# Three threshold searches of a top-k feed-forward layer: keys from PSUM, work moved into the rounds, one unit for the upper half

## The reference, cut to what matters

```python
input_acts_seq = gelu(einsum('bsd,nd->bsn', x, input_patterns)).mean(axis=1)     # (8, 2048)
top_input_acts, top_input_idx = top_k(input_acts_seq, 256)
input_repr = zeros((B, 2048)).at[brow, top_input_idx].set(top_input_acts)
process_acts = gelu(einsum('bn,pn->bp', input_repr, process_input_weights))      # (8, 1024)
top_process_acts, top_process_idx = top_k(process_acts, 128)
process_weights = softmax(top_process_acts, axis=-1)
aggregated_value = einsum('bk,bkd->bd', process_weights, process_values[top_process_idx])
output_acts_seq = gelu(einsum('bd,od->bo', aggregated_value, output_input_weights))   # (8, 2048)
top_output_acts, top_output_idx = top_k(output_acts_seq, 256)
out_per_seq = einsum('bk,bkm->bm', top_output_acts, output_patterns[top_output_idx])
x = x + tanh(g_ffn[1]) * broadcast(out_per_seq)
```

## Time and profile before

| | |
|---|---|
| median of 3 runs | 554.09 us (553.89 to 556.86) |
| profiled execution: time | 558.86 us |
| profiled execution: span, first to last instruction | 557.1 us |
| busy in the span | PE 377.0, DVE 380.4, ACT 264.1, POOL 105.8 us |
| mean granted TensorE clock | 0.825 of full |

### The profile page before, as it was taken

One profiled execution on the slowest core, in us unless ns is written; L12 is line 12 of the kernel. 1 busy time (PEld: TensorE's weight loads), 2 busy tenths in 40 slices (PEclk: granted clock), 3 DMA queues, 4 the chain that ended last, 5 costly groups with the idle time before them and its releaser, 6 DMA issues.

```text
span 557.1 us, 9426 instructions
## 1 busy us (share of the span) xinstructions
PE 377.0 (68%) x3000; PEld 251.6 (45%) x3004; DVE 380.4 (68%) x1614; ACT 264.1 (47%) x672; POOL 105.8 (19%) x384
## 2 busy tenths in 40 slices
PE   2899799912228699976998798898999601703006
PEld 2558576611116465563566566676545300203003
DVE  6643999989993767897887376581454576185773
ACT  3853544542222366545576375777453353253540
POOL 6694000000006239300495040000000000000000
PEclk9999599955556979999999798899999955855556
DMA  9800002459300597700759877900993000000002
GB/s 270 251 1 2 0 2 74 148 100 173 86 1 18 140 138 144 165 1 8 133 104 141 144 126 114 223 15 2 384 384 99 0 1 2 0 1 2 1 0 66
DMA packets 38585, 51.00 MB, mean 92 GB/s; under 512 B 5960, under 2 KB 35081, under 8 KB 37385
## 3 DMA queue, kind: packets, MB, share of 16 engines
q1 hardware_dynamic: 38537, 50.41, 38.9%
HBM read 40.28 MB, written 9.97 MB: 90 GB/s over the span
## 4 chain that ended last, share of the span: by engine, by line
PE 34%; DVE 33%; ACT 11%; DMA 7%; SPq 5%; issue 5%; POOL 4%; DVEq 0%; ACTq 0%; POOLq 0%
PE ps L2239 8%; DVE PR L1115 5%; ACT below L1829 5%; PE ps L2071 4%; DMA key_parts<-kp 4%; DVE R L1049 3%; PE ps L2016 2%; DVE below L1452 2%; DVE prod L1111 2%; PE ps L1932 2%; SPq L614 2%; SPq L628 2%; PE ps L2363 2%; PE ps L2189 2%; DVE PR L1113 2%
## 5 line engine op out<-in xcount | busy, mean ns | idle before, releaser
L1329 DVE TENSOR_REDUCE negm<-ps 112x1 f32<-112x375 f32 x128 | 64.0, 543 | 28.1 <-PE ps L2178 27.5
L1797 ACT ACTIVATE E<-ps 125x448 f32<-125x448 f32 x96 | 49.4, 546 | 28.1 <-PE ps L2189 26.1
L830 POOL CAST kp<-kx 128x188 bf16<-128x188 f32 (+1 forms) x32 | 10.6, 374 | 161.6 <-ACT path L1675 122.3
L1317 DVE TENSOR_REDUCE acts<-gel 128x4 f32<-128x448 f32 x32 | 19.8, 621 | 30.9 <-ACT gel L1761 30.9
L2203 PE MATMUL ps<-E,v 125*32 125x112 f32 x768 | 31.9, 274 | 5.8 <-issue 5.7
L2330 PE MATMUL ps<-cnt,same 128*128 128x7 bf16 (+1 forms) x22 | 3.6, 166 | 47.1 <-ACT below L1829 43.6
L2178 PE MATMUL ps<-ks,qs 96*112 96x375 bf16 x96 | 31.7, 347 | 4.0 <-DMA ks<-key_parts 2.9
L2189 PE MATMUL ps<-qs,ks 99*125 99x112 bf16 x288 | 30.5, 232 | 4.3 <-ACT E L1797 2.0
L2189 PEld LDWEIGHTS ps<-qs,ks 99*125 99x125 bf16 x288 | 27.2, 146 | 11.1 <-ACT E L1797 7.7
L1761 ACT ACTIVATE gel<-ps 128x448 f32<-128x448 f32 x32 | 17.3, 544 | 29.3 <-PE ps L2239 29.3
L1115 DVE TENSOR_TENSOR_SCAN PR<-UU,PR,prod 128x94 bf16<-128x94 bf16 x63 | 26.1, 414 | 2.2
(11 more groups left out here) (384 smaller groups left out, 1046.7 us busy)
## 6 DMA issues: line engine op xcount, KB each, us to landing
piwT<-fn_process_input_weights SPq DMA_DIRECT2D x4, 2048.0 KB, 17.0
ks<-key_parts SPq DMA_DIRECT2D x36, 187.5 KB, 7.9
key_parts<-kp SPq DMA_DIRECT2D x48, 93.8 KB
ctx_again<-in_ctx SPq DMA_DIRECT2D x7, 512.0 KB
keys<-kx SPq DMA_DIRECT2D x16, 187.5 KB, 2.0
kx<-keys SPq DMA_DIRECT2D x8, 375.0 KB, 7.1
ks_last<-key_parts SPq DMA_DIRECT2D x12, 187.5 KB, 6.8
ctxP<-in_ctx SPq DMA_DIRECT2D x8, 256.0 KB, 6.2
```

Of the source, the lines that this page charges most:

```text
L1317: dve.tensor_reduce(a0[:, i % NIT // 4, HB * half:HB * half + HB, i % 4], gel[:, i % 2, :].rearrange("p (b s) -> p b s", b=HB), AX.X, ALU. ...
L1329: drain(dve.tensor_reduce(negm[:, n:n + 1], bank(nm)[0:S, 0:SC], AX.X, ALU.max, negate=True), nm)
L1797: drain(fn(E[:, (KCH * f + c) % 6, :], bank(nm)[0:KC, 0:4 * S], ACT.Exp), nm)
```

## The change

The change touches the three searches alone. It does five things:

1. The copy of the transposed activations to `aT` is taken off the way to the keys: `sgn` and `key` read PSUM directly. Search 0 still makes the copy, in the wait of its round 0; search 1 makes none, since it never uses `aT`. The limits in `most` and the first `bound` are set before the activations are waited for.
2. The lower bits (`low`, `klo`) are made in the wait of round 0, not before the first round.
3. `khi` is stored in units of the lowest key bit (times 2^LOW), and so are `bound` and the candidates of the upper half. `kval` then is one instruction, (`khi` - `bound`) + `klo`.
4. The first candidates of the lower half come from a tile of their own, `low_cand`, written in the wait of round 1.
5. The softmax maximum of search 1 is spread over the waits of rounds 0, 1, 2 and 4 of that search, and its two PE instructions stand behind the counts of rounds 0 and 2. ACT's exponential moves behind ACT's tests of all rounds of search 1.

```diff
+                did(dve.memset(bound[:, :], -float(2 ** 31)))
                 if k < 2:
-                    nm = ("actT", k)
-                    wait_filled(dve, nm)
-                    drain(dve.tensor_copy(aT[:, :], bank(nm)[:, 0:128]), nm)
-                    wait_drained(dve, nm)
+                    turned_acts = ("actT", k)
+                    wait_filled(dve, turned_acts)
+                    bits = bank(turned_acts)[:, 0:128].bitcast(I32)
...
-                did(tt(key[:, :], sgn[:, :], bits, ALU.bitwise_xor))
+                ins = tt(key[:, :], sgn[:, :], bits, ALU.bitwise_xor)
...
                 did(dve.tensor_single_scalar(sgn[:, :], key[:, :], LOW[k], ALU.arith_shift_right))
-                did(dve.tensor_single_scalar(low, key[:, :], 2 ** LOW[k] - 1, ALU.bitwise_and))
-                settle()
-                did(dve.tensor_copy(khi[:, :], sgn[:, :]))
-                did(dve.tensor_copy(klo[:, :], low))
+                settle()
+                did(ts(khi[:, :], sgn[:, :], unit, None, ALU.mult))
                 settle()
                 first = sum(ROUNDS[:k])
-                ts(cand[:, 0:n], table(0)[0], -float(2 ** (31 - LOW[k])), None, ALU.add).then_inc(cand_ready, 1)
+                ts(cand[:, 0:n], table(0)[0], unit, -float(2 ** 31), ALU.mult, ALU.add).then_inc(cand_ready, 1)
                 dve.wait_ge(cand_ready, first + 1)
+
+                def beside(r):
+
+                    if r == 0:
+                        did(dve.tensor_single_scalar(low, key[:, :], 2 ** LOW[k] - 1, ALU.bitwise_and))
+                        settle()
+                        did(dve.tensor_copy(klo[:, :], low))
+                        if k == 0:
+                            drain(dve.tensor_copy(aT[:, :], bank(turned_acts)[:, 0:128]), turned_acts)
+                    if r == 1:
+                        lowest = [e[0] for e in rounds(k)].index(1)
+                        did(ts(low_cand[:, 0:n], table(lowest)[0], table(lowest)[1], None, ALU.mult))
+                    if k != 1:
+                        return
+                    if r == 0:
+                        dve.wait_ge(acts_ready, 2)
+                        dve.tensor_reduce(pmx[:, :], cells(acts[1], NPT), AX.X, ALU.max).then_inc(pmx_ready, 1)
+                    if r == 1:
+                        wait_filled(dve, "pmaxT")
+                        drain(dve.tensor_reduce(pm8[:, :], bank("pmaxT")[0:B, 0:128], AX.X, ALU.max), "pmaxT")
...
                 for r, (half, width, mine, theirs, last) in enumerate(rounds(k)):
...
-                    if half == 1 and r and rounds(k)[r - 1][0] == 0:
-
-                        did(ts(kval[:, :], khi[:, :], bound[:, 0:1], float(2 ** LOW[k]), ALU.subtract, ALU.mult))
-                        settle()
-                        val = kval[:, :]
-                        did(tt(val, val, klo[:, :], ALU.add))
-                        did(dve.memset(bound[:, :], 0.0))
-                        settle()
-                        ts(cand[:, 0:n], table(r)[0], table(r)[1], None, ALU.mult).then_inc(cand_ready, 1)
-                        dve.wait_ge(cand_ready, first + r + 1)
+                    if half == 1 and rounds(k)[r - 1][0] == 0:
+
+                        val, tried = kval[:, :], low_cand
+                        stt(val, khi[:, :], bound[:, 0:1], klo[:, :], ALU.subtract, ALU.add).then_inc(cand_ready, 1)
+                        dve.wait_ge(cand_ready, first + r + 1)
+                        did(dve.memset(bound[:, :], 0.0))
...
+                    beside(r)
                     nm = ("count", k, r)
                     wait_filled(dve, nm)
```

More of the change, by code:

```diff
@@ L423, in build_program @@
         nextb = r1.take("nextb", [128, 8])
+        low_cand = r1.take("low_cand", [128, 8])
         cnt = r1.take("cnt", [128, 8], BF16)
@@ L1432, in largest @@
+                if k == 1:
+                    drain(ins, turned_acts)
+                    wait_drained(dve, turned_acts)
+                else:
+                    did(ins)
+                    settle()
+                did(dve.tensor_single_scalar(sgn[:, :], key[:, :], LOW[k], ALU.arith_shift_right))
+                settle()
+                did(ts(khi[:, :], sgn[:, :], unit, None, ALU.mult))
                 settle()
                 first = sum(ROUNDS[:k])
-                ts(cand[:, 0:n], table(0)[0], -float(2 ** (31 - LOW[k])), None, ALU.add).then_inc(cand_ready, 1)
+                ts(cand[:, 0:n], table(0)[0], unit, -float(2 ** 31), ALU.mult, ALU.add).then_inc(cand_ready, 1)
@@ L1459, in largest @@
                         units, scale = table(r + 1)
-                        did(ts(nextb[:, 0:n], units, scale, bound[:, 0:1], ALU.mult, ALU.add))
+                        did(ts(nextb[:, 0:n], units, scale if half else scale * unit, bound[:, 0:1], ALU.mult, ALU.add))
+                    beside(r)
                     nm = ("count", k, r)
@@ L1517, in _ @@
                 drain(ins, nm)
[L1518 to L1523, removed]
-            ts(pmd[:, :], ident[0:B, 0:B], pm8[:, 0:1], None, ALU.mult).then_inc(pmd_ready, 1)
-            wait_filled(dve, "pmaxb")
-            drain(tt(cells(esel, NPT), cells(acts[1], NPT),
-                     bank("pmaxb")[:, 0:B].unsqueeze(2).broadcast_to([128, B, NPT]), ALU.subtract), "pmaxb")
             largest(1, B * NPT, NP // 8)
@@ L1826, in signs @@
                 val = kval if half else khi
+                tried = low_cand if half and rounds(k)[r - 1][0] == 0 else cand
                 with nc.allow_low_precision(reason="sums of signs up to 128 are exact"):
                     for m in range(mine, mine + theirs):
-                        ins = fn(below[:, m, :], val[:, :], ACT.Sign, bias=cand[:, m:m + 1], scale=-1.0,
+                        ins = fn(below[:, m, :], val[:, :], ACT.Sign, bias=tried[:, m:m + 1], scale=-1.0,
                                  accum_out=cnt[:, m:m + 1])
@@ L1846, in _ @@
             load_table(ACT.Exp)
+            for r in range(ROUNDS[1]):
+                signs(1, r)
             wait_drained(act, "pmaxb")
             fn(esel[:, :], esel[:, :], ACT.Exp).then_inc(pexp_ready, 1)
-            for r in range(ROUNDS[1]):
-                signs(1, r)
             load_table(ACT.Gelu)
@@ L2373, in _ @@
                 fill(ins, nm)
-            claim(pe, "pmaxT")
-            pe.wait_ge(pmx_ready, 1)
-            fill(tr(bank("pmaxT")[0:B, 0:128], pmx[:, :], ident[:, :]), "pmaxT")
-            claim(pe, "pmaxb")
-            pe.wait_ge(pmd_ready, 1)
-            fill(mm(bank("pmaxb")[:, 0:B], ones[0:B, :], pmd[:, :], start=True, stop=True), "pmaxb")
             act_transpose(1)
@@ L2382, in _ @@
                 count(1, r)
+                if r == 0:
+                    claim(pe, "pmaxT")
+                    pe.wait_ge(pmx_ready, 1)
+                    fill(tr(bank("pmaxT")[0:B, 0:128], pmx[:, :], ident[:, :]), "pmaxT")
+                if r == 2:
+                    claim(pe, "pmaxb")
+                    pe.wait_ge(pmd_ready, 1)
+                    fill(mm(bank("pmaxb")[:, 0:B], ones[0:B, :], pmd[:, :], start=True, stop=True), "pmaxb")
             ties(1)
```

25 lines of the change are left out of this document (16 added, 9 removed).

## The result

The changed kernel took 548.61 us (median of 4 executions, 545.3 to 550.58), the kernel before 554.71 in the same comparison (4, 553.89 to 556.86). The ratio is 0.988 with a 95% interval of 0.9838 to 0.9922. The forecast was 4.1 us, a ratio of 0.9926. Over all comparisons, this one included, the changed kernel has a mean of 549.6 us (23 executions) and the kernel before 554.6 (116): 5.0 us less, give or take 1.1 (95%, from the scatter of the single executions), about 0.9%. Three executions far outside the others, at 580 to 973 us, are left out here and in all means.

What follows compares the result with a forecast made beforehand. No engine alone but the dependent chain through the searches was taken to bound the kernel. Savings 1.45 + 1.47 + 1.55 less 0.35 lost gave 4.12 us; 554.09 - 4.1 = 550.0 us, range 548.2 to 552.2.

Steps and rivals of the forecast that it cites:

- A, keys: Key steps ahead of each search's first test: 0.55, 0.55 and 0.35 us saved, 1.45 in all, between 1.03 and 1.69.
- The surcharge for PSUM: Keys of searches 0 and 1: reading PSUM adds 0.06 us each to `sgn` and `key`.
- B, switch: From `bound` to the first lower test, each search: 1.07 us becomes 0.58, saving 0.49 three times, 1.47 in all.
- C, softmax maximum: Between `acts` and search 1: the wait of 2.03 us becomes 0.48, so search 1 starts 1.55 us earlier.
- The table load: ACT's load for Exp ahead of search 1: stays hidden by 0.40 us; the rival that it shows had under 0.02.
- D, the waits: Work moved into DVE's waits: 0.20 us lost in search 0, 0.1 and 0.05 in search 1; 0.35 in all.
- Rival 2: Clock rise in product L2363 shifts by 3 us: 1.5 us either way, 551.5 or 548.5; spread L2426 likewise; chance 0.20.
- L: Follow-up theory, not forecast: clock rises in product and end meet the shorter tail better, about 1 us beyond the searches' 4.4.
- S: Follow-up theory, not forecast: only the searches got faster, 4.4 us; the rest is scatter between executions.
- T: Follow-up theory, not forecast: the change gains more than its parts in every execution, first put at 6 to 8 us.
- d/2: Product L2363: a clock rise d later after the product's start costs d/2, since half speed does half the work.

Runs made afterwards that it cites:

- shared_out: Changed kernel with search 0's copy moved to the wait of round 2 and the `klo` cast to round 3; ratio 0.9883 to the kernel before.
- the delays: Settings of an unused tile ahead of search 0: eight in the kernel before, ratio 1.003; twelve in the changed kernel, ratio 0.9954.
- the first control: The kernel before, unaltered, under a label of its own (also written control); ratio 1.0052 to the kernel before, mean 556.8 us beside 553.6.
- again2: The changed kernel, unaltered, timed a third time; ratio 0.9909 to the kernel before.
- before_late: The kernel before with eight settings of an unused tile ahead of the first key step of search 0; ratio 1.003 to the kernel before.

## Why the prediction fell short

*A, keys.* Foreseen 0.55, 0.55 and 0.35; measured 0.61, 0.61 and 0.34. The surcharge for PSUM was taken twice and holds once. The Trainium skill, "VectorE: DVE Perf Modes", "The perf-mode tier table (the rule you actually need)", says that two-tensor operations on fp32 have only the slowest mode, in SBUF too. `key`, on int32 of the same width, fits that: it stayed at 0.29. The higher fixed cost of PSUM that the prediction cited does not show in `key`, and against the 0.20 us for each search that it estimated from those figures stand 0.06 measured.

*B, switch.* Foreseen 0.49 three times, measured 0.49, 0.48 and 0.49.

*C, softmax maximum.* Foreseen 1.55, measured 1.55 (2.03 to 0.48). The table load stayed hidden, by 0.34 us.

*D, the waits.* Foreseen 0.20, 0.10 and 0.05; measured 0.19, 0.09 and 0. shared_out shows that even these can be had back.

*Sum.* Foreseen 4.12, measured 4.44 in the searches. 0.11 of the difference is in A and 0.07 in D, 0.01 the other way in B. Of the remaining 0.15, 0.09 are in round 9 of search 0, where a pause of DVE moved behind the candidates (last section); the rest is spread over hundredths. Each step of the mechanism was right, and the sizes to a few hundredths.

*What failed is the step from the sum to the time:* "the stretches used above do not scale with it, so I take 4.1 off the median". It took the medians of a few executions as if they were fixed, and put all that happens outside the searches at nothing. In the first pair of traces 9.0 us were measured: 4.4 in the searches, 2.5 ahead of them, and 2.1 in the product and the end. Executions of the kernel before spread from 548.7 to 562.4 us. The traces show two sources in code that the change leaves alone: what runs ahead of the scaling (435.6 to 442.5 us at its end; up to 2.2 us of that have arisen by 278 us, the rest by 373, and from 382 on the traces run in step) and the place of the clock's rises. Rival 2 named the second, with 1.5 us for the product (L2363 took 8.8 us instead of 9.3), and left its price in the spread, some 1.9 us between the two levels, without a number. The first had no term at all. A median of 3 or 4 such executions is uncertain by 1 us or more on each side, and the range, 2 us wide on either side, had been spent on the terms of the sum. Over 23 and 116 executions the gain is 5.0 with 3.9 to 6.1, which holds the forecast and the sum alike. So the 6 us of the first comparison were in part chance: four executions each, the changed kernel's with a mean of 548.3, 1.3 under that of all its executions.

*What stays open.* 5.0 measured less 4.4 in the searches leaves 0.6 us, no more than its uncertainty. The tails of three traces on each side differ by 5.1 us (114.9 and 109.9 from the scaling to the end): 4.4 in the searches, 0.1 in the product, 0.5 in the end. That would fit L, but one lower level in three traces is no proof, and the delays did not confirm it. Without the first comparison, which raised the question, the gain is 4.7 (19 executions at 549.8, 112 at 554.6), give or take 1.2, still nearer to S. T in its first form, with 2 us or more beyond the parts, would need 6.4 or more and lies outside both intervals. Those intervals come from single executions; the first control shows that a whole label can lie 2 to 3 us off, so this is unlikely rather than excluded. Why the maximum alone gave 3.3 us by its ratio, where its trace has 1.57 in the searches, was not settled.

## What to carry to other kernels

In a chain of short dependent instructions, start-to-start distances from the timeline give the gain of a change to a few hundredths of a microsecond, and work moved into a wait is free until the instructions' spacing, not their durations, fills it. Compare such a change by the stretch it touches: here the searches of one program repeat to 0.02 us while whole executions differ by several microseconds. Look at what the clock does ahead of each dense product: matmuls whose results nobody reads, in PE's idle waits, took the product and the end together from 23.6 us (mean of the three traces of the changed kernel) to 18.5 (mean of two), 5.1 less, more than all the edits of the searches (4.4).

## What the runs showed of the hardware beyond that

- DVE's independent instructions can start 0.14 us apart though each takes 0.22 to 0.28: in the changed round 0 `eq` at 443.27, 0.14 after `nextb`, and the copy at 443.66, 0.14 after `klo`.
- Some candidates (L1473, L1501 after the change) start about 0.35 us late without any wait that ends there. In round 9 of search 0 before, they start 0.63 after the comparison, in nearly all other rounds 0.28:

```profile
466.85 0.17 DVE L1468 SCALAR_TENSOR_TENSOR reached<-ps,most 128x7 f32<-128x7 f32 x1 [0.31 <-PE ps L2330]
467.48 0.17 DVE L1473 SCALAR_TENSOR_TENSOR cand<-nsel,nextb 128x7 f32<-128x7 f32 x1 [0.45 <-DVE reached L1468]
```

  DVE's list of waits puts 0.9 us and two cases on it in the kernel before and in control (rounds 0 and 9 of search 0), 0.5 and one case in the changed kernel and in again2 (round 0), and none in shared_out. The pause has not gone there: in round 9 after the change it lies between the candidates and `bound` (0.39 us where 0.08 is usual), and in shared_out also behind the candidates of round 0, ahead of DVE's first test (0.36 us after `bound` where 0.12 is usual). So it belongs to a place in the program, moves by single instructions when the list changes, and costs less behind the candidates. Its cause was not tested; no DMA packet of any kind, code included, falls into the two pauses of the kernel before (446.3 to 447.5 and 466.3 to 467.6 us). In before_late it took 0.7 us out of search 0 and put 0.35 into search 2, which is why a delay of 2.07 us (441.99 - 439.21 = 2.78 to the copy, 0.71 before) lengthened search 0 by 1.37 only.
- Each microsecond by which the clock rises later in the product costs 0.49 us (10.15 to 11.79 us for rises 2.5 to 5.8 us behind its start), as d/2 had it.
